# Four decoder layers in one kernel: weighing two head pairs at a time, a feed-forward in rounded halves, and a rotation that reads PSUM first

## Chip, cores and metric

One core of a Trainium2 chip runs the whole program in one launch. Its engines are TensorE (PE; its weight loads are shown as PEld), VectorE (DVE), ScalarE (ACT), GpSimd (POOL) and SyncE (SP, which here issues nearly all DMAs). Each works through its own list of instructions in order and waits on semaphores. The metric is the device time in microseconds.

## What is computed

Four cross-attention layers, one after the other, on x (16 samples of 100 rows of 256) against one context (16 samples of 361 rows of 256), all in fp32:

```python
x = L0(x, ctx)   # LayerNorm of x and ctx, 16 heads of 16, residual; then a feed-forward
x = L1(x, ctx)   # RMS norm of x, 16 heads of 64, residual
x = L2(x, ctx, mask)   # rotary keys and queries, mask, 16 heads of 64, residual, LayerNorm
x = L3(x, ctx)   # LayerNorm of x and ctx, 16 heads of 16, residual

# the feed-forward at the end of L0
y = layer_norm(x, ln2_g, ln2_b)
y = gelu(y @ w1 + b1)          # 256 -> 1024
x = x + (y @ w2 + b2)          # 1024 -> 256

# the rotation in L2, applied to keys and queries
x1, x2 = x[..., 0::2], x[..., 1::2]
r1, r2 = x1 * cos - x2 * sin, x2 * cos + x1 * sin
```

## The kernel before

The program has four parts in a row: `narrow_layer("L0")`, `feed_forward()`, `wide_layers()` for L1 and L2, `narrow_layer("L3")`. Between parts all engines meet.

**Products of halves.** A product of fp32 numbers is made of rounded halves in most places: an operand's high half is its value rounded to fp32r (ACT writes it), the low half is the rest (DVE subtracts), and PE sums high·high, high·low and low·high with moving operands in fp32r. Transposes, weighing and output projections take fp32 operands as they are; the trace shows each fp32 product as two records.

**Narrow part.** A slot (s, q) handles four heads of sample s: `turn(g-1, 0)`, `scores`, the jobs of list `a_`, `turn(g-1, 1)`, the jobs of `b_`. `jobs_at(s, q)` says which jobs: K, Q, V projections of the next samples, P (weighing), N, M, O (the way to the output). All jobs write into two banks PJ in turn, so job n waits until job n-2 has been read (`taken`). M is read by ACT (`L_OT<-PJ`), O by DVE (`X<-PJ,X`). On ACT a slot's order is: unload, two exponentials, `a_`, two exponentials, `b_`. On DVE: two maxima, the N job, unload, everything else.

**Feed-forward.** Groups of 4 samples (400 columns). PE makes the hidden layer from halves of W1 (line 972, 8 tiles of 128 rows, 6 products each), ACT applies gelu, PE makes the output with 100 rows of one sample as the stationary side and W2 in fp32 as the moving side (line 981, 8 products of 256 columns for each sample), ACT copies it, DVE adds it and the bias to X. A hardware loop runs over the groups; all of a group's hidden tiles come ahead of its output.

**Wide part.** 32 samples in a row (16 of L1, then 16 of L2) by 8 slots (s, p), a slot being two heads of 64. On PE a slot is: `scores(s, p)`, the jobs of `after_scores` (K of the next sample), `turn(g-1)` (transposes of the exponentials), `after_turn`, `weigh(g-2)`, `after_weigh`. Jobs share three banks. Q jobs exist in odd samples alone (two samples at a time), so samples come in pairs, an even one and an odd one. `scores` works on 64 rows, `weigh` on 64 columns of the array at a time. `weigh` of p = 0 and 4 must wait until `scale` (DVE, `wide_OT<-PS,wide_OT`, in slots 2 and 6) has read the bank PO. V is kept once, so V jobs wait for the weighings that read it.

In L2 each K and Q is rotated: ACT copies it out of PSUM (`wide_T`), DVE swaps neighbouring rows (`stream_shuffle`, into `wide_SH`), POOL makes two products (`wide_AC`, `wide_SH`), DVE adds them one slot later (`join`), ACT rounds the sum (`wide_KH`, `wide_QH`), DVE makes the low half (`wide_KL`, `wide_QL`). At p = 0 of each sample POOL also makes the tables of the next one (`tables`: mask times cos and sin). The raw context C has two slots, so SP loads two samples ahead.

## Time and profile before

| | |
|---|---|
| median of 3 runs | 2268.0 us (2266.34 to 2273.81) |
| the profiled run, its own time | 2268.11 us |
| its span in the profile | 2266.2 us, mean granted clock 0.963 |
| PE / PEld busy | 2062.2 us (91%) / 1678.8 us (74%) |
| DVE / ACT / POOL busy | 1425.7 us (63%) / 1263.5 us (56%) / 581.4 us (26%) |
| start of the parts, us | L0 0, feed-forward 370, wide 481, L3 1926 |

The span runs from the first to the last instruction of the profile. Busy PE time is not PE at its peak, since matmuls overlap: their pace is read from the distance of their starts. POOL's spans are rough. What stands in brackets or after "|" behind a row, with "<-", is the idle time of the engine ahead of it and who ended it.

### The profile page before, as it was taken

What the parts mean: (1) busy time and instruction counts of PE and PEld (TensorE: products, weight loads), DVE (VectorE), ACT (ScalarE), POOL (GpSimd) and SP (SyncE); (2) the same over time, 40 slices, a digit from 0 to 9 for tenths busy, and PEclk for the clock granted to TensorE, in tenths of its full rate; (3) what the DMA queues carried; (4) which work ended last, traced back from release to release, by engine and by line L of the source; (5) the groups of instructions that cost most, each with busy time, mean ns of one, the idle gap of its engine ahead of it and who ended that gap; (6) DMA issues with size and microseconds to landing.
All of it is one profiled execution on the core that took longest, in us unless ns stands there. A gap on an engine that the chain in (4) does not pass through costs nothing. (4 is left out here: it accounts for less than half of the span.)

```text
span 2266.2 us, 50658 instructions
## 1 busy us (share of the span) xinstructions
PE 2062.2 (91%) x18696; PEld 1678.8 (74%) x18696; DVE 1425.7 (63%) x2880; ACT 1263.5 (56%) x3225; POOL 581.4 (26%) x676
## 2 busy tenths in 40 slices
PE   6888986979999999999989999899999998889897
PEld 5777775867787787787767777777777776777776
DVE  5777774335445455454587777777777775577775
ACT  3677774335555555555555555555555554577775
POOL 3232320000000000000055655655556551000000
PEclk8999997989999999999999999999999999799999
DMA  6444332011000000000001000000000000344432
GB/s 170 135 136 139 117 122 82 0 52 58 14 8 8 14 8 15 8 8 14 9 15 35 15 9 9 9 9 15 9 9 10 1 1 1 115 121 121 121 122 71
DMA packets 72965, 109.69 MB, mean 48 GB/s; under 512 B 7062, under 2 KB 62618, under 8 KB 72730
## 3 DMA queue, kind: packets, MB, share of 16 engines
q1 hardware_dynamic: 72442, 105.98, 15.4%
q8 instruction: 155, 2.54, 0.5%
q14 instruction: 80, 0.66, 0.1%
q10 hardware_dynamic: 288, 0.51, 0.1%
HBM read 69.28 MB, written 37.19 MB: 47 GB/s over the span
## 5 line engine op out<-in xcount | busy, mean ns | idle before, releaser
L1444 ACT ACTIVATE wide_P<-PS,MX 100x361 f32<-100x361 f32 x512 | 288.9, 564 | 415.3 <-DVE MX L1562 411.4
L1562 DVE TENSOR_REDUCE MX<-PS 100x2 f32<-100x722 f32 x256 | 231.5, 904 | 181.4 <-PE PS L1312 181.3
L626 ACT ACTIVATE L_P<-PS,MX 100x361 f32<-100x361 f32 x512 | 253.5, 567 | 132.2 <-DVE MX L752 132.2
L752 DVE TENSOR_REDUCE MX<-PS 100x2 f32<-100x722 f32 x256 | 219.9, 900 | 48.3 <-PE PS L512 47.7
L1738 POOL TENSOR_TENSOR wide_AC<-wide_T,wide_COSM 128x362 f32<-128x362 f32 x128 | 118.0, 922 | 409.4 <-DVE wide_SH L1520 408.1
L1335 PE MATMUL PS<-wide_PT,wide_V 128*64 128x100 f32 (+1 forms) x3072 | 189.1, 257 | 29.6 <-issue 29.6
L524 PE MATMUL PP<-CON,L_P 100*128 100x100 f32 x1536 | 183.9, 257 | 26.6 <-DVE L_PT L759 20.7
L1335 PEld LDWEIGHTS PS<-wide_PT,wide_V 128*64 128x64 f32 (+1 forms) x3072 | 139.4, 136 | 84.4 <-issue 68.2
L524 PEld LDWEIGHTS PP<-CON,L_P 100*128 100x128 f32 x1536 | 151.5, 144 | 47.8 <-ACT L_P L626 34.3
L1321 PE MATMUL PP<-CON,wide_P 100*128 100x100 f32 x1536 | 179.6, 254 | 0.8 <-ACT wide_PT L1451 0.5
L1321 PEld LDWEIGHTS PP<-CON,wide_P 100*128 100x128 f32 x1536 | 164.6, 144 | 10.4 <-issue 2.0
L1418 ACT ACTIVATE wide_V<-PJ 128x512 f32<-128x512 f32 (+1 forms) x127 | 76.4, 601 | 153.7 <-PE PJ L1234 152.8
L1699 POOL TENSOR_TENSOR VE<-MV 128x2 f32<-128x2 f32 x8 | 2.5, 306 | 577.2 <-DVE MV L1615 577.2
L1234 PE MATMUL PJ<-wide_CTH,wide_WH 128*128 128x362 f32 x342 | 134.8, 394 | 2.9 <-DVE wide_KL L1515 1.6
L1739 POOL TENSOR_TENSOR wide_SH<-wide_SH,wide_SINM 128x362 f32<-128x362 f32 x128 | 133.8, 1045 | 0.0
L1568 DVE COPY wide_PT<-PP 128x300 f32<-128x300 f32 x256 | 116.6, 456 | 0.0
L1234 PE MATMUL PJ<-wide_WH,wide_CTH 128*128 128x512 f32 (+1 forms) x254 | 112.6, 443 | 4.2 <-ACT wide_T L1393 4.2
L1234 PE MATMUL PJ<-wide_CTH,wide_WL 128*128 128x362 f32 x342 | 116.0, 339 | 0.0
L1234 PE MATMUL PJ<-wide_CTL,wide_WH 128*128 128x362 f32 x342 | 115.9, 339 | 0.0
L759 DVE COPY L_PT<-PP 128x600 f32<-128x600 f32 x128 | 99.4, 777 | 18.6 <-PE PP L524 14.4
L1451 ACT ACTIVATE wide_PT<-PP 128x300 f32<-128x300 f32 x256 | 108.9, 425 | 0.6 <-PE PP L1321 0.6
L1532 DVE TENSOR_TENSOR wide_KL<-wide_AC,wide_KH 128x362 fp32r<-128x362 f32 x128 | 106.2, 830 | 0.9 <-ACT wide_KH L1401 0.3
(255 smaller groups left out, 5434.4 us busy)
## 6 DMA issues: line engine op xcount, KB each, us to landing
strips<-L_KS SPq DMA_DIRECT2D x256, 90.5 KB
L_KA<-strips SPq DMA_DIRECT2D x64, 362.0 KB, 3.1
C<-ctx_t SPq DMA_DIRECT2D x32, 361.0 KB, 3.1
kept<-L_CTH SPq DMA_DIRECT2D x16, 361.0 KB, 4.9
kept<-L_CTL SPq DMA_DIRECT2D x16, 361.0 KB, 5.5
L_CTH<-kept SPq DMA_DIRECT2D x16, 361.0 KB, 4.3
L_CTL<-kept SPq DMA_DIRECT2D x16, 361.0 KB, 5.1
C<-in_ctx SPq DMA_DIRECT2D x16, 256.0 KB, 3.4
```

Of the source, the lines that this page charges most:

```text
L524: last = nc.tensor.transpose(PPB[:, n, SQ * t:SQ * t + SQ], P[:, (4 * g + 2 * i + n) % 8, 128 * t:128 * t + 128], ident[0:SQ, 0:SQ])
L626: nc.scalar.activation(P[:, (4 * g + j) % 8, 0:SK], PSB[0:SQ, j, 0:SK], ACT.Exp, bias=MX[:, s % 2, 4 * q + j:4 * q + j + 1], scale=1.0).th ...
L752: nc.vector.tensor_reduce(MX[:, s % 2, 4 * q + 2 * i:4 * q + 2 * i + 2], PSB[0:SQ, 2 * i:2 * i + 2, 0:SK], AX.X, ALU.max, negate=True).the ...
L1234: last = nc.tensor.matmul(dst, l, r, start=n == 0, stop=n == len(todo) - 1)
L1321: last = nc.tensor.transpose(PP[i][:, SQ * t:SQ * t + SQ], P[:, (2 * g + i) % 4, 128 * t:128 * t + 128], ident[0:SQ, 0:SQ])
L1335: last = nc.tensor.matmul(PO[64 * i:64 * i + 64, SQ * at:SQ * at + SQ], V[0:r, 1024 * c + 64 * h:1024 * c + 64 * h + 64], PT[0:r, (2 * g + ...
L1444: nc.scalar.activation(P[:, (2 * g + i) % 4, 0:SK], PS_[i][0:SQ, 0:SK], ACT.Exp, bias=MX[:, s % 2, h:h + 1], scale=1.0, accum_out=DEN[:, s ...
L1451: nc.scalar.activation(PT[:, (2 * g + 1) % 4, :], PP[1][:, 0:KV_TILES * SQ], ACT.Copy).then_inc(Z["unloaded_odd"], 1)
L1562: nc.vector.tensor_reduce(MX[:, s % 2, 2 * p:2 * p + 2], PSB[0:SQ, 0:2, 0:SK], AX.X, ALU.max, negate=True).then_inc(Z["maxed"], 1)
L1568: nc.vector.tensor_copy(PT[:, (2 * g) % 4, :], PP[0][:, 0:KV_TILES * SQ]).then_inc(Z["unloaded_even"], 1)
L1738: nc.gpsimd.tensor_tensor(ac, src, c, ALU.mult)
L1739: nc.gpsimd.tensor_tensor(sh, sh, t, ALU.mult).then_inc(Z["rotated"], 1)
```

## The change

- **Narrow parts.** On ACT the M job is put ahead of a slot's exponentials. On DVE the O job is put ahead of the unload.
- **Feed-forward.** Unrolled; hidden tiles and output run as one stream, tile u of the hidden layer ahead of the output product of tile u-2. W2 and the gelu's result are split into halves too, the output is made transposed (256 rows of 400 columns, 6 products of 400 columns for each tile), gets its bias on ACT (`b2` is now a column vector), is transposed back (`back`) and added by DVE out of PSUM. W1's split is done in two halves.
- **Wide parts.** `weigh` runs in odd slots for two slots at once (g-3 and g-2), PT has 6 buffers in place of 4, `after_weigh` is gone and its V jobs are in other slots, O moves from p = 3 to 5. The wait for Wo moves from the start of the part to the first projection. C has one slot: SP loads context(s+1) once sample s has been split, so context(1) comes behind the load of L2's weights.
- **Rotation.** DVE swaps rows straight from PSUM, then ACT copies, then POOL makes both products and their sum. `post_stats` and `post` move from p = 4, 6 to 6, 7.

```diff
--- before.py
+++ after.py
+                        for key in a_:
+                            if key[0] == "M":
+                                job(key)
...
-                            job(key)
+                            if key[0] != "M":
+                                job(key)
...
                         for key in a_:
-                            if key[0] == "N":
+                            if key[0] in "NO":
                                 job(key)
                         if turns:
                             unload(g - 1)
                         for key in a_ + b_:
-                            if key[0] != "N":
+                            if key[0] not in "NO":
                                 job(key)
...
+                    def hidden(u):
+                        i, t = divmod(u, nf)
+                        pe.wait_ge(Z["w1_low"], 1 + 2 * t // nf)
+                        pe.wait_ge(Z["y_low"], KE * (i + 1))
+                        if u >= 2:
+                            pe.wait_ge(Z["hid_taken"], u - 1)
+                        c = slice(128 * t, 128 * t + 128)
+                        todo = [x for k in range(KE) for x in ((W1H[:, k, c], YH[:, i % 2, k, :]), (W1H[:, k, c], YL[:, i % 2, k, :]),
+                                                               (W1L[:, k, c], YH[:, i % 2, k, :]))]
+                        for m, (x, y) in enumerate(todo):
+                            last = nc.tensor.matmul(hid[u % 2][:, 0:GS], x, y, start=m == 0, stop=m == len(todo) - 1)
+                        last.then_inc(Z["hid_made"], 1)
+
+                    def output(u):
+                        i, t = divmod(u, nf)
+                        pe.wait_ge(Z["w2_low"], 1)
+                        pe.wait_ge(Z["hid_low"], u + 1)
+                        if t == 0 and i >= 2:
+                            pe.wait_ge(Z["out_taken"], KE * (i - 1))
                         for k in range(KE):
-                            bank = begin(i, n0 + k)
-                            for g in range(G):
-                                last = nc.tensor.transpose(bank[:, SQ * g:SQ * g + SQ], YN[:, g, 128 * k:128 * k + 128], ident[0:SQ, 0:SQ])
-                            last.then_inc(S["product"], 1)
-
-                    turn(0, 0, 0)
-                    pe.wait_ge(S["low_w"], 1)
-
-                    def body(i, last_group):
-                        pe.wait_ge(S["split"], i * KE + KE)
-                        for t in range(nf):
-                            bank = begin(i, HID + t)
-                            todo = [x for k in range(KE) for lh, ll in [[W[:, FF * k + 128 * t:FF * k + 128 * t + 128] for W in (WH, WL)]]
-                                    for x in ((lh, YH[:, k, :]), (lh, YL[:, k, :]), (ll, YH[:, k, :]))]
-                            for m, (x, y) in enumerate(todo):
-                                last = nc.tensor.matmul(bank[:, 0:G * SQ], x, y, start=m == 0, stop=m == len(todo) - 1)
-                            last.then_inc(S["product"], 1)
-                        if not last_group:
-                            turn(i, TURN, i + 1)
-                        pe.wait_ge(wo_in["ffn"], 16)
-                        pe.wait_ge(S["taken"], i * per + (HID + nf + nb))
+                            c = slice(128 * k, 128 * k + 128)
+                            for m, (x, y) in enumerate(((W2H, HH), (W2H, HL), (W2L, HH))):
+                                last = nc.tensor.matmul(outs[i % 2][k][:, 0:GS], x[:, t, c], y[:, u % 4, :], start=t == 0 and m == 0,
+                                                        stop=t == nf - 1 and m == 2)
+                        last.then_inc(Z["out_made"], 1)
...
+                    def back(i, half):
+                        pe.wait_ge(Z["out_taken"], KE * (i + 1))
+                        if i + 2 < groups:
+                            pe.wait_ge(Z["gained"], KE * (i + 2) + half + 1)
+                        else:
+                            pe.wait_ge(Z["added"], G * (i - 1) + 2 * half + 2)
+                        for v in range(2):
+                            g = 2 * half + v
+                            for k in range(KE):
+                                last = nc.tensor.transpose(turns[half][0:SQ, E * v + 128 * k:E * v + 128 * k + 128],
+                                                           OT[:, k, SQ * g:SQ * g + SQ], ident)
+                        last.then_inc(Z["back_made"], 1)
...
+                    for u, i, t in stream():
+                        if u < U:
+                            hidden(u)
+                        if u >= 2:
+                            output(u - 2)
+                        if i + 1 < groups and t in (3, 4):
+                            turn(i + 1, t - 3)
+                        if 0 < i < groups and t in (5, 6):
+                            back(i - 1, t - 5)
+                    for half in range(2):
+                        back(groups - 1, half)
...
+                    def hidden(u):
+                        act.wait_ge(Z["hid_made"], u + 1)
+                        if u >= 3:
+                            act.wait_ge(Z["hid_low"], u - 2)
+                        nc.scalar.activation(H32[:, u % 3, :], hid[u % 2][:, 0:GS], ACT.Gelu, bias=col("b1", u % nf)).then_inc(Z["hid_taken"], 1)
+                        act.wait_ge(Z["hid_taken"], u + 1)
+                        if u >= 4:
+                            act.wait_ge(Z["out_made"], u - 3)
+                        nc.scalar.activation(HH[:, u % 4, :], H32[:, u % 3, :], ACT.Copy).then_inc(Z["hid_high"], 1)
...
+                    stats(0)
+                    moments(0)
+                    split_w1(0)
                     normalise(0)
-                    split(0, 0, 0)
...
+                    split_w1(1)
+                    for k in range(KE):
+                        split(0, k)
+                    dve.wait_ge(Z["w2_high"], 1)
+                    nc.vector.tensor_tensor(W2L[:, :, :], w2, W2H[:, :, :].bitcast(fp32), ALU.subtract).then_inc(Z["w2_low"], 1)
...
-                after_scores, after_turn, after_weigh = [], [], []
+                after_scores, after_turn = [], []
                 if s + 1 < NS:
                     after_scores.append(("K", s + 1, p))
                 if s % 2 and s + 1 < NS:
                     after_turn.append(("X", s + 2, 0))
                 if p == 1 and s > 0:
                     after_turn.append(("R", s - 1, 1))
-                if p == 3 and s > 0:
+                if p == 5 and s > 0:
                     after_turn.append(("O", s - 1, 0))
                 if p == 5 and s < NS:
                     after_turn.append(("R", s, 0))
-                if p in (3, 4, 5) and s < NS:
-                    after_turn.append(("V", s, 3 + p - 3))
-                if p in (5, 6, 7) and s + 1 < NS:
-                    after_weigh.append(("V", s + 1, p - 5))
-                return after_scores, after_turn, after_weigh
-
-            SLOTS = [(s, p) for s in range(NS) for p in range(HP)] + [(NS, p) for p in range(4)]
+                if p in (2, 3, 4) and s < NS:
+                    after_turn.append(("V", s, 3 + p - 2))
+                if p in (6, 7) and s + 1 < NS:
+                    after_turn.append(("V", s + 1, p - 6))
+                if p == 0 and 0 < s < NS:
+                    after_turn.append(("V", s, 2))
+                return after_scores, after_turn
+
+            SLOTS = [(s, p) for s in range(NS) for p in range(HP)] + [(NS, p) for p in range(6)]
...
                     context(0)
-                    context(1)
                     load_output_weights(sp, "L1")
                     sp.wait_ge(Z["padded"], 1)
                     mask(B)
                     sp.wait_ge(Z["w_low"], 5)
                     load_weights(sp, "L2")
                     for s in range(NS):
-                        if s + 2 < NS:
+                        if s + 1 < NS:
                             sp.wait_ge(Z["c_low"], KE * (s + 1))
-                            context(s + 2)
+                            context(s + 1)
...
+                        if s == 0:
+                            pe.wait_ge(wo_in["L1"], 16)
...
-                        if 2 <= g <= HP * NS + 1:
+                        if g % 2 and 3 <= g <= HP * NS + 1:
+                            weigh(g - 3)
                             weigh(g - 2)
-                        for key in after_weigh:
-                            job(key)
 
...
-                        act.wait_ge(Z["made"], job_no[key] + 1)
+                        act.wait_ge(Z["shuffled"], r + 1)
                         if r >= NT:
                             act.wait_ge(Z["rotated"], r - NT + 1)
                         nc.scalar.activation(T32[:, r % NT, 0:n], bank(key)[:, 0:n], ACT.Copy).then_inc(Z["copied"], 1)
...
-                        dve.wait_ge(Z["copied"], r + 1)
-                        nc.vector.stream_shuffle(SH[:, r % NB, 0:n], T32[:, r % NT, 0:n], [q ^ 1 for q in range(32)]).then_inc(Z["shuffled"], 1)
-
-                    def join(key):
-                        n, r = (SKE if key[0] == "K" else 2 * SQ), turn_no[key]
-                        dve.wait_ge(Z["rotated"], r + 1)
-                        nc.vector.tensor_tensor(AC[:, r % NB, 0:n], AC[:, r % NB, 0:n], SH[:, r % NB, 0:n], ALU.add).then_inc(Z["joined"], 1)
+                        dve.wait_ge(Z["made"], job_no[key] + 1)
+                        nc.vector.stream_shuffle(SH[:, r % NB, 0:n], bank(key)[:, 0:n], [q ^ 1 for q in range(32)]).then_inc(Z["shuffled"], 1)
...
+                        shuffles_first = s + 1 < NS and rope(s + 1)
+                        if shuffles_first:
+                            for key in after_scores:
+                                job(key)
                         if p == 2 and s:
                             scale(s - 1, 1)
                         if p == 6 and s < NS:
                             scale(s, 0)
-                        for key in turns_of(g - 1):
-                            join(key)
...
-                        pool.wait_ge(Z["shuffled"], r + 1)
+                        pool.wait_ge(Z["copied"], r + 1)
...
                         nc.gpsimd.tensor_tensor(sh, sh, t, ALU.mult).then_inc(Z["rotated"], 1)
+                        pool.wait_ge(Z["rotated"], r + 1)
+                        nc.gpsimd.tensor_tensor(ac, ac, sh, ALU.add).then_inc(Z["joined"], 1)
```

ACT in a narrow part, the slot q = 3 of a sample in L3 (L_PT: unload, L_P: exponentials, L_OT: the M job). Before:

```order
2170 L633 ACTIVATE L_PT<-PP 128x600
2171 L626 ACTIVATE L_P<-PS,MX 100x361 x2
2172 L575 ACTIVATE L_OT<-PJ 128x200
2173 L575 ACTIVATE L_V<-PJ 105x16x16
2174 L626 ACTIVATE L_P<-PS,MX 100x361 x2
```

Now:

```order
2204 L622 ACTIVATE L_PT<-PP 128x600
2205 L564 ACTIVATE L_OT<-PJ 128x200
2206 L615 ACTIVATE L_P<-PS,MX 100x361 x2
2207 L564 ACTIVATE L_V<-PJ 105x16x16
2208 L615 ACTIVATE L_P<-PS,MX 100x361 x2
```

The eviction of M stands one place earlier, ahead of the first two exponentials.

PE in L2, slot p = 2 of an even sample, from the transposes to the next scores (wide_MNEG). Before:

```order
4415 L1321 MATMUL PP<-CON,wide_P 128x100 x6
4416 L1335 MATMUL PS<-wide_PT,wide_V 64x100 x6
4417 L1309 MATMUL PS<-wide_MNEG,wide_FILL 100x362 x2
4418 L1312 MATMUL PS<-wide_KH,wide_QH 100x362 x2
4419 L1312 MATMUL PS<-wide_KL,wide_QH 100x362 x2
```

Now:

```order
4607 L1395 MATMUL PP<-CON,wide_P 128x100 x6
4608 L1306 MATMUL PS<-wide_WH,wide_CTH 128x512
4609 L1306 MATMUL PS<-wide_WL,wide_CTH 128x512
4610 L1306 MATMUL PS<-wide_WH,wide_CTL 128x512
4611 L1306 MATMUL PS<-wide_WH,wide_CTH 128x512
4612 L1306 MATMUL PS<-wide_WL,wide_CTH 128x512
4613 L1306 MATMUL PS<-wide_WH,wide_CTL 128x512
4614 L1383 MATMUL PS<-wide_MNEG,wide_FILL 100x362 x2
```

The weighing that stood in slot 2 is gone to slot 3, and a V job stands in its place.

DVE in L2, slot p = 2 of an odd sample (wide_OT: scale; wide_AC: join). Before:

```order
1189 L1562 TENSOR_REDUCE MX<-PS 100x2
1190 L1584 TENSOR_TENSOR wide_OT<-PS,wide_OT 128x400
1191 L1525 TENSOR_TENSOR wide_AC<-wide_AC,wide_SH 128x362
1192 L1525 TENSOR_TENSOR wide_AC<-wide_AC,wide_SH 128x200
1193 L1520 STREAM_SHUFFLE wide_SH<-wide_T 128x362
1194 L1568 COPY wide_PT<-PP 128x300
1195 L1520 STREAM_SHUFFLE wide_SH<-wide_T 128x200
1196 L1532 TENSOR_TENSOR wide_KL<-wide_AC,wide_KH 128x362
1197 L1535 TENSOR_TENSOR wide_QL<-wide_AC,wide_QH 128x200
```

Now:

```order
1164 L1629 TENSOR_REDUCE MX<-PS 100x2
1165 L1592 STREAM_SHUFFLE wide_SH<-PJ 128x362
1166 L1651 TENSOR_TENSOR wide_OT<-PS,wide_OT 128x400
1167 L1635 COPY wide_PT<-PP 128x300
1168 L1592 STREAM_SHUFFLE wide_SH<-PS 128x200
1169 L1599 TENSOR_TENSOR wide_KL<-wide_AC,wide_KH 128x362
1170 L1602 TENSOR_TENSOR wide_QL<-wide_AC,wide_QH 128x200
```

Both joins are gone from DVE (POOL has them now), and the shuffle of K reads the PSUM bank and stands ahead of scale.

## Rows read from the trace of the kernel before

**Rows 1.** busy time by stretch: length, PE PEld DVE ACT POOL busy, clock, DMA.
```profile
516.00:1125.00 609.00, 601.53 (x4814) 480.01 (x4812) 304.67 (x600) 320.57 (x936) 12.65 (x32) 1.00 0.04 11
1175.00:1885.00 710.00, 654.74 (x5105) 527.85 (x5104) 529.35 (x1148) 380.07 (x1113) 415.17 (x443) 0.95 0.04 11
1362.81:1407.75 44.94, 40.99 (x321) 32.52 (x321) 33.52 (x67) 23.85 (x68) 24.35 (x25) 0.96 0.05 10
1407.75:1458.42 50.67, 47.47 (x366) 38.88 (x365) 37.77 (x91) 27.03 (x81) 31.62 (x37) 0.93 0.04 10
1377.28:1380.69 3.41, 3.41 (x17) 2.89 (x14) 3.41 (x4) 0.95 (x3) 1.80 (x2) 0.50 0.00 0
1408.00:1413.00 5.00, 5.00 (x49) 4.24 (x46) 4.52 (x12) 2.95 (x9) 4.86 (x5) 1.00 0.01 3
```

**Rows 2.** groups by line, narrow stages: what | busy, mean | idle before.
```profile
L372 PE MATMUL PJ<-L_CTH,L_WH 128*128 128x362 f32 x128 | 49.1, 384 | 24.9 <-ACT L_OT L575 23.7 <-DVE L_CTL L696 1.1
...
L372 PE MATMUL PJ<-L_XTH,L_WH 128*128 128x200 f32 x128 | 38.9, 304 | 23.1 <-DVE X L719 19.6 <-DVE L_XTL L696 2.4 <-DVE L_QB L700 0.8
```

**Rows 3.** timeline, last narrow stage: start, length, engine, what [idle before].
```profile
2062.91 1.02 ACT L626 ACTIVATE L_P<-PS,MX 100x361 f32<-100x361 f32 x2 [0.81 <-DVE MX L752]
2063.82 0.34 ACT L575 ACTIVATE L_OT<-PJ 128x200 f32<-128x200 f32 x1
...
2069.09 0.77 DVE L759 COPY L_PT<-PP 128x600 f32<-128x600 f32 x1
2069.78 0.41 DVE L719 TENSOR_TENSOR X<-PJ,X 100x256 f32<-100x256 f32 x1
```

**Rows 4.** timeline of PE in the feed-forward, first group of samples.
```profile
388.13 0.34 PE L972 MATMUL PP<-ffn_YH,ffn_WH 128*128 128x400 f32 x1
...
388.31 0.34 PE L972 MATMUL PP<-ffn_YL,ffn_WH 128*128 128x400 f32 x1
...
398.35 3.40 PEld L981 LDWEIGHTS PS<-WO,ffn_HT 128*100 128x100 f32 x16
```

**Rows 5.** timeline: first and last of the feed-forward block.
```profile
370.75 1.91 ACT L989 ACTIVATE ffn_WH<-W_RAW 128x2048 fp32r<-128x2048 f32 x1 [1.93 <-PEq L280]
...
383.55 0.69 PE L972 MATMUL PS<-ffn_YH,ffn_WH 128*128 128x400 f32 x1 [2.09 <-DVE ffn_YL L1038]
...
481.41 1.06 ACT L1372 ACTIVATE wide_WH<-W_RAW 128x1024 fp32r<-128x1024 f32 x1 [1.21 <-PEq L936]
```

**Rows 6.** timeline and DMA list: start of the wide stage.
```profile
485.95 0.61 DVE L1623 TENSOR_SCALAR wide_XN<-X,RS 100x256 f32<-100x256 f32 x2
...
489.89 0.93 PE L1264 MATMUL PJ<-CON,wide_XN 100*128 100x100 f32 x4 [10.12 <-DMA WO<-in_L_xattn_wo]
...
515.99 0.89 ACT L1380 ACTIVATE wide_CTH<-C 128x361 fp32r<-128x361 f32 x2
...
W_RAW<-in_L_xattn_Wq SPq DMA_DIRECT2D x1, 1024.0 KB, 10.3
```

**Rows 7.** timeline of PE, layer 1: one weighing, then scores.
```profile
801.01 0.74 PE L1335 MATMUL PS<-wide_PT,wide_V 128*64 128x100 f32 x12
801.68 0.41 PE L1312 MATMUL PS<-wide_KH,wide_QH 64*100 64x362 f32 x2
```

**Rows 8.** groups by line, 15 samples of layer 2: waits and rotation.
```profile
L1739 POOL TENSOR_TENSOR wide_SH<-wide_SH,wide_SINM 128x362 f32<-128x362 f32 x120 | 125.1, 1042 | 0.0
...
L1532 DVE TENSOR_TENSOR wide_KL<-wide_AC,wide_KH 128x362 fp32r<-128x362 f32 x121 | 100.9, 834 | 0.7
...
L1335 PE MATMUL PS<-wide_PT,wide_V 128*64 128x100 f32 x960 | 67.7, 261 | 24.5 <-issue 24.5
...
L1309 PE MATMUL PS<-wide_MNEG,wide_FILL 64*100 64x362 f32 x240 | 50.8, 415 | 24.9 <-ACT wide_P L1444 24.9
...
L1739 POOL TENSOR_TENSOR wide_SH<-wide_SH,CON 128x200 f32<-128x200 f32 x57 | 42.1, 739 | 0.0
```

**Rows 9.** groups by line, 15 samples of layer 1: the same subtraction without GpSimd.
```profile
L1515 DVE TENSOR_TENSOR wide_KL<-PJ,wide_KH 128x362 fp32r<-128x362 f32 x78 | 41.7, 535 | 65.1 <-ACT wide_KH L1385 65.1
```

294 lines of the change are left out of this document (159 added, 135 removed).

## The prediction

> **What bounds the kernel now.** I read the page's busy times first: PE is busy 91% of the span, DVE 63%, ACT 56%, POOL 26%. Then the windows by stage [rows 1]. In 15 samples of layer 1, PE works 601.5 of 609.0 us at full clock and POOL almost not at all: only shorter PE work helps there. In 15 samples of layer 2, 710.0 us go by for nearly the same products. The difference has three places: PE idles 24.5 us ahead of weighings and 24.9 us ahead of scores [rows 8], and the granted clock is 0.95; part of each sample is at 0.50, the 1.2 GHz level [rows 1]. A mean of 0.95 is a tenth of the time at half speed, which costs about 35 us. An even sample took 44.9, an odd one 50.7 us. For narrow stages and feed-forward I read groups by line and the timeline: which wait ends last ahead of PE.
>
> **Narrow stages.** PE's K and Q products idle behind two readers of their bank, 23.7 us behind ACT's copy of M and 19.6 behind DVE's add of O [rows 2]: 43.3 us in 32 samples, 1.35 each. The timeline shows why [rows 3]. ACT waited 0.81 us for the maximum, ran two exponentials, and only then copied M. The copy (0.34 us) can now start when that wait began, at 2062.91 - 0.81 = 2062.10, 1.7 us earlier, and costs the exponentials nothing as long as M is made before the maximum. On DVE O's add (0.41 us) stood behind an unload of 0.77; it will end about 0.7 us earlier, and the unload and the turn that waits for it 0.4 later, a turn that comes later in PE's list. All 43.3 would be the upper end. Next late are exponentials and maxima, which these swaps don't make faster, so I take three quarters: **-32**; range -20 (only M's wait, less a little) to -43.
>
> **Feed-forward.** The block takes 481.41 - 370.75 = 110.7 us [rows 5]. Its hidden products start 0.18 us apart; the output of one sample takes 3.40 us [rows 4], so 13.6 per group of four, and nothing overlaps it. Now each tile has 6 hidden and 6 output products of 400 columns: a group is 8 x 12 x 0.18 = 17.3 us, and about 2.0 for 16 transposes there and back (four took 0.93 [rows 6], less in a row). Four groups make 77.2. ACT has two passes for each tile and DVE one, each of 400 columns; one tile lasts 2.18 us on PE, so both are hidden, by the lead of two tiles. If one tile's ACT work were over 2.18 us, 32 times the excess would show. The start: the first product came 12.8 us in [rows 5], behind a whole split of W1 (1.91 us on ACT, as much on DVE) ahead of the statistics. Half a split and statistics first give back about 4: 8.6. The end gets longer by the way back (copy, transposes, add): about 4.0 in all. W2's split stands on ACT and DVE before the first output, two tiles behind. 8.6 + 77.2 + 4.0 = 89.8: **-21** (-17 to -23).
>
> **Start of the wide stage.** PE waits 10.12 us for Wo and goes at 489.89, while x was normalised at 485.95 + 0.61 = 486.56 [rows 6]; 3.3 us can go. But context(1) now stands in SP's queue behind 3 MB of weights, each of which took 10.3 us to land [rows 6]. They are issued near 502.5; I put the landing at 513 to 514.5, and ACT would want it at 515.99 - 3.3 = 512.7. Up to 1.8 us comes back: **-1.5** (-3.3 to +2).
>
> **Layer 1.** A weighing takes 801.68 - 801.01 = 0.67 us with entry and exit of its column mode [rows 7]; two take 1.34. Entry and exit are now paid once for two weighings, and products change to them once instead of twice. What that is worth no row shows by itself; it lies between 0 and 0.67 us a pair, and I estimate 0.24, a third of one weighing, since most of the 0.67 must be its 12 records: 0.24 x 4 a sample, 15 us a layer. The V product no longer follows a weighing, and V jobs fill slots in which PE waited for the softmax: I take 0.6 us a sample, another 9. **-24** (-15, if only the pairing counts at my price, to -26). In this layer DVE and ACT have half their time free (304.7 and 320.6 of 609 us [rows 1]).
>
> **Layer 2.** (a) Pairing as in layer 1: -24. (b) In slot 2 the weighing waited for `scale`; 24.5 us in 15 samples [rows 8], 26 in 16. It now comes a slot later, with a V job between: -26. (c) The joins. DVE loses them, which it needn't (529 of 710 us busy). POOL gets a third pass. Its price isn't in the trace: the nearest row is the second product, 1.04 us for K and 0.74 for Q [rows 8], same sizes and operands, and I take these. Below it the subtraction of the same size on an engine with free ports, 0.53 [rows 9]; above it, 2.0 if an add of two late operands waits for DVE each time. POOL's work goes from 24.4 to 24.4 + 8 x 1.04 = 32.7 us in an even sample and from 31.6 to 31.6 + 8 x 1.78 = 45.9 in an odd one. PE's floor (length less clock loss, less 3.3 of waits, less 1.6 by (a)) is about 38 even and 42 odd. So POOL is the bound of odd samples, by some 4 us, and not of even ones. Inside a sample the queue is uneven: at p = 0 the tables take 4.86 of 5 us [rows 1], and K and Q of p = 0 to 2 stand behind them. What waits is ACT's rounding, and ACT is in order: its next exponentials stand behind it, and PE's scores behind these. Placing the passes one after another by these durations, I get a stall of 2.3 to 2.9 us near p = 3 in each sample, where PE idles 24.9 / 15 = 1.7 us now [rows 8]: with odd samples' excess +15. (d) The shuffle out of PSUM takes a copy out of the chain, which shortens it, and frees the bank later, which three banks cover: 0. (e) The clock: what stands before each half-clock stretch is idle PE. One idle place of the two goes, one stays, so I leave the dips: 0, with up to -35 if they vanish. Sum **-35**; range +20 (joins at 1.5 and 1.1: odd samples near 52) to -75.
>
> In trace rows the same subtraction into KL takes 834 ns beside a busy POOL [rows 8] and 535 without [rows 9]. The Trainium skill has a rule that speaks against the joins: "Perfetto Trace Analysis", section "Optimizing Scalar/DVE Operations", says that GpSimd and DVE share a read port of SBUF, so that work moved between them might not help; "SBUF — State Buffer", section "Who interferes with whom", says that a DVE instruction with two SBUF inputs contends with a GpSimd one that reads SBUF. The rows agree with it.
>
> **The last samples** of the wide stage lose two weighings' entries: -1. **Sum**: -32 - 21 - 1.5 - 24 - 35 - 1 = -114.5. The profiled run's span is 2266.2 us with 1.9 outside it; its 2268.11 is the median 2268.0. 2266.2 - 114.5 + 1.9 = 2153.6: **2154 us**.
>
> **Rivals.** *B: POOL's queue takes layer 2's gain.* With POOL busy 39 of 47 us a sample instead of 28, each subtraction with two SBUF operands meets it more often: the 0.30 us between 834 and 535 [rows 8, 9] came at a share of 415 / 710 = 0.58, and 0.83 would make it 0.43; POOL's passes grow alike, to about 1.3 and 0.95, and odd samples stay near 50. Layer 2 gains nothing: 2154 + 35 = **2189**. For it: POOL is the bound of odd samples even at my price. Against: DVE reads memory less often itself (no joins, shuffles from PSUM). This is what the Trainium skill's rule on the shared port would give. *C: both stalls and the dips go.* If POOL's queue is drained before anyone waits, layer 2 runs at layer 1's pace and clock, -95 instead of -35: about **2095**. For it: one idle place of two goes for certain. Against: the tables at p = 0. *E: the swaps in the narrow stages only move the wait* to the scores: -10 there, about **2176**. For it: exponentials and maxima hold PE elsewhere already. *D: slower.* The one mechanism is the price of the joins. Everything outside layer 2 gives -79.5, so layer 2 must lose that much, 10.6 us a pair of samples. With even samples at 43, an odd one must reach 63, which is 31.6 + 8 x 3.9: the joins of K and Q must cost 3.9 us together, where the rows give 1.78. At 2.5 and 1.8 us the odd sample is 66.0, the pair 109 against 95.6, 7.5 pairs lose 100: **2289**. Only a pass twice as dear as its neighbour does it.
>
> **Chances.** A (the forecast) 0.50, B 0.20, C 0.17, E 0.08, D 0.05. The forecast's own terms spread over 2130 to 2175. The range 2100 to 2210 takes in B and E with their spread and half of C; left out are half of C, the far end of B and D, under 2 in 10. Faster by over 0.3% (about what a measurement of this kernel can tell from no change): A, C, E and all of B but 0.02, so 0.93; within 0.3%: 0.02 of B, 0.01 of D, so 0.03; slower: 0.04.
>
> **What the new profile would show.** Narrow: the idle time of K and Q products behind the copy of M and the add to X gone; if it names the exponentials instead, E. Feed-forward: output products 0.18 us apart, block near 90 us. Wide start: no wait for Wo, and ACT's first split of context(1) released by a DMA. Layer 1: 24 weigh records in about 1.1 us, two samples in 78.5 where 609 / 7.5 = 81.2 are now. Layer 2: the wait ahead of weighing gone; POOL's third pass near 1.04 and 0.74 us; ACT's rounding released by POOL, scores late near p = 3 once a sample; odd samples 45.6 to 48.3, even 42.9 to 44.4; dips at 0.50 still there. The forecast fails most easily on the join's price and on the clock.

## The result and the profile after

| | before | changed |
|---|---|---|
| median | 2270.7 us (4 runs) | 2143.1 us (4 runs, 2141.1 to 2145.4) |
| span of the profiled run, mean clock | 2266.2 us, 0.963 | 2139.7 us, 0.975 |

The ratio is 0.944, with a 95% interval of 0.9417 to 0.9462. The forecast was 2154 us. The parts, each from one profiled execution of either kernel; a sample begins with its first scores product, and sample 15 is the last of layer 1:

| part | forecast, us | measured, us |
|---|---|---|
| first narrow stage | -16 | 370.75 to 353.75: -17.0 |
| feed-forward | -21 | 110.7 to 90.9: -19.7 |
| start of the wide stage, to sample 0 | -1.5 | 33.97 to 32.28: -1.7 |
| layer 1, samples 0 to 14 | -24 (16 samples) | 609.7 to 589.2: -20.5 |
| samples 15 to 30 | -35 (layer 2, 16 samples) | 760.2 to 700.7: -59.5 |
| the rest with the last narrow stage | -17 (-16 and -1) | 381.0 to 372.8: -8.2 |

The windows of the changed kernel are first layer 1, then layer 2, then an even and an odd sample of layer 2 (length, then PE, PEld, DVE, ACT, POOL busy, clock, DMA). They answer to [rows 1].

```profile
477.00:1066.00 589.00, 582.57 (x4813) 474.68 (x4812) 305.51 (x600) 321.31 (x937) 12.59 (x32) 0.99 0.04 11
1114.00:1767.00 653.00, 610.64 (x5106) 499.52 (x5106) 456.26 (x966) 376.60 (x1111) 538.29 (x620) 1.00 0.05 13
1375.49:1417.24 41.75, 38.46 (x322) 31.02 (x321) 27.84 (x55) 23.17 (x68) 30.43 (x34) 1.00 0.06 12
1417.24:1463.08 45.84, 43.35 (x368) 35.96 (x366) 33.74 (x77) 27.27 (x84) 42.29 (x52) 1.00 0.04 10
```

Two samples of layer 2 take 87.6 us where 95.6 were, and the clock there is 1.00 where it was 0.95. POOL is busy 42.3 us of an odd sample.

Groups of PE, both narrow stages together, beside [rows 2]:

```profile
L361 PE MATMUL PJ<-L_CTH,L_WH 128*128 128x362 f32 x128 | 49.5, 387 | 4.9 <-DMA L_CTL<-kept 3.7 <-DVE L_CTL L689 1.1
...
L361 PE MATMUL PJ<-L_XTH,L_WH 128*128 128x200 f32 x128 | 39.1, 305 | 11.9 <-DVE X L712 6.7 <-DVE L_XTL L689 2.6 <-DVE L_QB L693 1.6
```

The wait behind ACT's copy of M is gone, that behind O's add is 6.7 instead of 19.6 us. 3.7 us behind a DMA (`L_CTL<-kept`) are new, all in the last stage. The exponentials are hardly named more than before: PE's transposes idle 6.9 us behind them where it was 4.2.

Feed-forward and the start of the wide stage, timeline, beside [rows 4 to 6]:

```profile
353.75 2.00 ACT L1016 ACTIVATE ffn_W1H<-W_RAW 128x1024 fp32r<-128x1024 f32 x2 [1.93 <-PEq L269]
...
363.09 0.67 PE L958 MATMUL PJ<-ffn_YH,ffn_W1H 128*128 128x400 f32 x1 [2.10 <-DVE ffn_YL L1089]
...
368.08 0.34 PE L970 MATMUL PS<-ffn_HH,ffn_W2H 128*128 128x400 f32 x1
...
368.26 0.34 PE L970 MATMUL PS<-ffn_HL,ffn_W2H 128*128 128x400 f32 x1
```

```profile
444.67 1.06 ACT L1444 ACTIVATE wide_WH<-W_RAW 128x1024 fp32r<-128x1024 f32 x1 [2.45 <-PEq L936]
...
450.20 0.90 PE L1336 MATMUL PJ<-CON,wide_XN 100*128 100x100 f32 x4 [6.85 <-DVE wide_XN L1690]
```

Output products are 0.18 us apart like the hidden ones; the first hidden product comes 9.34 us in (12.8 before; I had put 8.6), and the block ends at 444.67. In the wide stage PE no longer waits for Wo, but for x. ACT's split of context(1) starts at 477.55 with no idle time ahead of it, so the DMA wait that I had named as a sign isn't there.

A pair of weighings in layer 1, beside [rows 7], takes 1.19 us, where two single ones took 1.34:

```profile
794.55 1.26 PE L1409 MATMUL PS<-wide_PT,wide_V 128*64 128x100 f32 x24
795.74 0.41 PE L1386 MATMUL PS<-wide_KH,wide_QH 64*100 64x362 f32 x2
```

Layer 2, groups by form: GpSimd's third pass for K and Q, the subtraction, ACT's rounding, the mask product ahead of scores, beside [rows 8]:

```profile
L1811 POOL TENSOR_TENSOR wide_AC<-wide_AC,wide_SH 128x362 f32<-128x362 f32 x120 | 122.1, 1017 | 9.4
...
L1811 POOL TENSOR_TENSOR wide_AC<-wide_AC,wide_SH 128x200 f32<-128x200 f32 x57 | 37.3, 655 | 4.5
...
L1599 DVE TENSOR_TENSOR wide_KL<-wide_AC,wide_KH 128x362 fp32r<-128x362 f32 x121 | 93.4, 771 | 76.4 <-ACT wide_KH L1473 76.4
...
L1473 ACT ACTIVATE wide_KH<-wide_AC 128x362 fp32r<-128x362 f32 x120 | 61.1, 509 | 12.6 <-POOL wide_AC L1811 12.6
...
L1383 PE MATMUL PS<-wide_MNEG,wide_FILL 64*100 64x362 f32 x242 | 49.5, 398 | 41.7 <-ACT wide_P L1516 41.7
```

The third pass costs 1.02 and 0.66 us, where I had taken 1.04 and 0.74 from the second pass. An even sample takes 41.8 us (forecast: 42.9 to 44.4), an odd one 45.8 (45.6 to 48.3). The 24.5 us ahead of the weighing are gone, and the wait ahead of scores has grown from 24.9 to 41.7 us. One such wait, in slots 2 and 3 of an even sample:

```profile
1385.28 0.41 PE L1383 MATMUL PS<-wide_MNEG,wide_FILL 64*100 64x362 f32 x2 [0.58 <-ACT wide_P L1516]
...
1385.51 0.96 POOL L1811 TENSOR_TENSOR wide_AC<-wide_AC,wide_SH 128x362 f32<-128x362 f32 x1
...
1386.50 0.51 ACT L1473 ACTIVATE wide_KH<-wide_AC 128x362 fp32r<-128x362 f32 x1 [1.47 <-POOL wide_AC L1811]
...
1387.04 0.75 DVE L1599 TENSOR_TENSOR wide_KL<-wide_AC,wide_KH 128x362 fp32r<-128x362 f32 x1 [2.76 <-ACT wide_KH L1473]
...
1387.71 0.89 DVE L1629 TENSOR_REDUCE MX<-PS 100x2 f32<-100x722 f32 x1
...
1388.64 0.56 ACT L1516 ACTIVATE wide_P<-PS,MX 100x361 f32<-100x361 f32 x1 [0.93 <-DVE MX L1629]
...
1390.44 0.41 PE L1383 MATMUL PS<-wide_MNEG,wide_FILL 64*100 64x362 f32 x2 [1.11 <-ACT wide_P L1516]
```

GpSimd's sum ends at 1386.47. ACT has waited 1.47 us for it, rounds, and only then can DVE subtract, after 2.76 us of nothing. The next maximum stands behind that subtraction on DVE: its scores had begun at 1385.28 and the maximum comes at 1387.71. So the exponentials are late, and the next scores by 1.11 us.

### The profile page after: what moved, and what is told of

It is laid out like the page before. It is cut to its first block and busy times, and to the rows that moved or that the text cites. A ratio compares the mean times of both kernels' runs of the same rounds, so it can differ in the third digit from the quotient of the medians.

```text
span 2139.7 us, 50608 instructions
## 1 busy us (share of the span) xinstructions
PE 1984.0 (93%) x18664; PEld 1642.6 (77%) x18664; DVE 1358.2 (63%) x2706; ACT 1269.3 (59%) x3249; POOL 720.1 (34%) x868
## 3 DMA queue, kind: packets, MB, share of 16 engines
q8 instruction: 157, 2.57, 0.5%
## 5 line engine op out<-in xcount | busy, mean ns | idle before, releaser
L1811 POOL TENSOR_TENSOR wide_AC<-wide_AC,wide_SH 128x362 f32<-128x362 f32 x192 | 172.0, 896 | 15.1
L1395 PEld LDWEIGHTS PP<-CON,wide_P 100*128 100x128 f32 x1536 | 160.3, 141 | 10.2 <-issue 2.8
L1409 PE MATMUL PS<-wide_PT,wide_V 128*64 128x100 f32 (+1 forms) x3072 | 160.9, 253 | 0.0
L1599 DVE TENSOR_TENSOR wide_KL<-wide_AC,wide_KH 128x362 fp32r<-128x362 f32 x128 | 97.9, 765 | 79.8 <-ACT wide_KH L1473 79.8
L1809 POOL TENSOR_TENSOR wide_SH<-wide_SH,wide_SINM 128x362 f32<-128x362 f32 x128 | 140.4, 1097 | 0.0
L1306 PE MATMUL PJ<-wide_CTH,wide_WH 128*128 128x362 f32 x340 | 130.5, 384 | 0.8 <-DVE wide_KL L1587 0.7
L1306 PE MATMUL PJ<-wide_WH,wide_CTH 128*128 128x512 f32 (+1 forms) x258 | 108.2, 420 | 0.0
```

The source lines that it names most:

```text
L1306: last = nc.tensor.matmul(dst, l, r, start=n == 0, stop=n == len(todo) - 1)
L1395: last = nc.tensor.transpose(PP[i][:, SQ * t:SQ * t + SQ], P[:, (2 * g + i) % 4, 128 * t:128 * t + 128], ident[0:SQ, 0:SQ])
L1409: last = nc.tensor.matmul(PO[64 * i:64 * i + 64, SQ * at:SQ * at + SQ], V[0:r, 1024 * c + 64 * h:1024 * c + 64 * h + 64], PT[0:r, (2 * g + ...
L1809: nc.gpsimd.tensor_tensor(sh, sh, t, ALU.mult).then_inc(Z["rotated"], 1)
L1811: nc.gpsimd.tensor_tensor(ac, ac, sh, ALU.add).then_inc(Z["joined"], 1)
```

## The experiments

Where a table gives stretches, they are those of the parts above: samples 0 to 14, and 15 to 30.

Each ratio is to executions of the kernel before that were taken together with that kernel; their medians were 2267.5, 2273.3 and 2274.1 us, so medians of different rows are comparable to a few microseconds.

| kernel | median, us | ratio to before, 95% interval | 0 to 14 | 15 to 30 |
|---|---|---|---|---|
| before | 2270.7 | | 609.7 | 760.2 |
| changed | 2143.1 | 0.944 (0.9417 to 0.9462) | 589.2 | 700.7 |
| narrow swaps alone, on before | 2246.7 | 0.9881 (0.9838 to 0.9924) | 609.0 | 765.3 |
| M alone, on before | 2258.0 | 0.9965 (0.9933 to 0.9997) | 610.1 | 762.6 |
| swap from PSUM alone, on before | 2220.8 | 0.9773 (0.971 to 0.9835) | 609.1 | 708.0 |
| changed, weighings apart | 2173.4 | 0.9575 (0.9548 to 0.9602) | 609.5 | 707.3 |
| changed, one weighing a slot | 2146.5 | 0.9463 (0.9436 to 0.9489) | 600.7 | 695.2 |
| changed, sums on DVE | 2116.8 | 0.9313 (0.9298 to 0.9329) | 593.1 | 671.5 |
| changed, sum twice on GpSimd | 2238.1 | 0.9856 (0.9838 to 0.9875) | 592.0 | 792.0 |
| changed, swap out of the copy | 2187.7 | 0.9619 (0.9596 to 0.9641) | 589.2 | 738.5 |
| changed, Q's sum on DVE | 2141.0 | 0.9419 (0.9403 to 0.9435) | 590.6 | 695.2 |
| sums on DVE, weights in small pieces | 2110.2 | 0.9295 (0.9237 to 0.9353) | 586.9 | 670.6 |
| the same, tables early | 2103.4 | 0.9265 (0.9205 to 0.9325) | 585.9 | 666.3 |
| the same, single weighing in layer 2 | 2106.3 | 0.9285 (0.9226 to 0.9344) | 586.8 | 668.9 |

**The narrow swaps.** Kernel before, plus the hunks on ACT and DVE:

```diff
                         if turns:
                             unload(g - 1)
+                        for key in a_:
+                            if key[0] == "M":
+                                job(key)
...
-                            if key[0] == "N":
+                            if key[0] in "NO":
```

> The kernel before with the two swaps of the narrow stages alone. The prediction says -32 (about 2236 us). The changed kernel's trace already shows -17 in the first narrow stage and about -9 in the last one, where 3.7 us are waits for a DMA (L_CTL<-kept): by it -26, about 2242. The rival that the swaps only move the wait gives -10, about 2258.

> The kernel before with the M job ahead of the exponentials on ACT, and O left where it was. If the two waits add up, this takes away the 23.7 us behind L_OT and leaves the 19.6 behind X: about -15, 2254 us. If O's late add makes good for it (one wait in the place of the other), the idle time behind X grows to 30 or more and the time falls by under 6.

PE's groups of the first kernel:

```profile
L372 PE MATMUL PJ<-L_CTH,L_WH 128*128 128x362 f32 x128 | 49.6, 387 | 8.3 <-DMA L_CTL<-kept 7.0 <-DVE L_CTL L700 1.1
...
L372 PE MATMUL PJ<-L_XTH,L_WH 128*128 128x200 f32 x128 | 37.8, 295 | 11.6 <-DVE X L723 6.4 <-DVE L_XTL L700 2.6 <-DVE L_QB L704 1.6
```

and of the second:

```profile
L372 PE MATMUL PJ<-L_CTH,L_WH 128*128 128x362 f32 x128 | 49.1, 383 | 2.0 <-DVE L_CTL L700 1.1 <-DMA L_CTL<-kept 0.8
...
L372 PE MATMUL PJ<-L_XTH,L_WH 128*128 128x200 f32 x128 | 39.5, 308 | 26.1 <-DVE X L723 21.7 <-DVE L_XTL L700 2.5 <-DVE L_QB L704 0.8
```

Both swaps gave 1.2% of 2267, 27 us (17 to 37); in the trace 11 in the first stage and 13.3 from the last samples on. The changed kernel's trace had led me to expect 26. M alone gave 8 us (1 to 15) by the ratio, a third of the vanished 23.7 us of wait; in its one trace the two narrow parts are 14 us shorter. That lies between what I expected if the waits add up (15) and if one takes the other's place (under 6). O's wait stayed, at 21.7. So the waits don't replace each other, but only a part of each is gained. With both swaps the last stage waits 3.7 to 7.0 us for the DMA of the kept context. Lengths of the first stage differ between kernels with the same code there (353.75 in the changed kernel, 356.62 with the sums on DVE), so single microseconds of it are not to be read.

**Weighing.** In the changed kernel, apart:

```diff
                         for key in after_scores:
                             job(key)
+                        if g % 2 and 3 <= g <= HP * NS + 1:
+                            weigh(g - 3)
                         if 1 <= g <= HP * NS:
                             turn(g - 1)
...
-                            weigh(g - 3)
                             weigh(g - 2)
```

and one in each slot:

```diff
-                        if g % 2 and 3 <= g <= HP * NS + 1:
-                            weigh(g - 3)
+                        if 2 <= g <= HP * NS + 1:
                             weigh(g - 2)
```

> The changed kernel with the two weighings of an odd slot apart: the first one ahead of the transposes, the second one at the slot's end. Everything else stands where it stood. If sharing the entry and exit of the column mode is what pays, it costs 1.34 - 1.19 us for the weighing and about 0.15 for the transposes or V product beside it: 0.3 x 4 x 32 = 38 us where nothing hides it, and 25 to 38 with layer 2's waits: 2168 to 2181. If the other places of V, O and weighing are what pays, under +8: 2143 to 2151.

> The changed kernel with one weighing in every slot, two slots back, as before the change; the other jobs stay in their new places. This brings back single weighings (+25 to +38) and the wait for scale in slots 2 and 6 of layer 2 (+26). If that wait's idle time is what lowered the granted clock in the kernel before, the clock of layer 2 falls from 1.00 to about 0.95 again, for 30 us more: about 2235. If the joins on DVE had lowered it, the clock stays at 1.00: about 2205.

The first expectation was met in its number (2173.4 of 2168 to 2181), but the second run shows that its reason was wrong. One weighing a slot was to cost 60 us or more; it costs 3 us in all, inside the noise. In layer 1 two samples take 79.7 us (81.9 before, 78.5 changed): 1.24 us by pairing, 0.155 for each of 8 pairs, and 2.1 by what else the change does there, the new places of V and O above all. In layer 2 single weighing is 5.5 us faster, in one trace of each. The wait for `scale` doesn't come back: ahead of the weighings PE waits 2.5 us in 15 samples (24.5 before), with a V job now ahead of the weighing in slot 2. The clock stays at 1.00; that the sums on DVE had lowered it, as this branch of the expectation says, is not so either, since below it is 1.00 with the sums on DVE. Apart but in the same slot is 30 us worse, 2.5 in two samples of layer 1: the first weighing then stands ahead of the transposes. Both of these runs have single weighings, and they differ by 1.3 us in two samples of layer 1: the place of a weighing counts for about as much as sharing its entry and exit.

**The rotation.** Sums back on DVE:

```diff
...
                         if p == 6 and s < NS:
                             scale(s, 0)
+                        for key in turns_of(g - 1):
+                            join(key)
...
                         nc.gpsimd.tensor_tensor(sh, sh, t, ALU.mult).then_inc(Z["rotated"], 1)
-                        pool.wait_ge(Z["rotated"], r + 1)
-                        nc.gpsimd.tensor_tensor(ac, ac, sh, ALU.add).then_inc(Z["joined"], 1)
```

> The changed kernel with both sums of the rotation on DVE again, one slot later, behind scale; the rest of the change stays. If POOL's queue makes the 5.8 us that scores still wait in two samples of layer 2, they shrink and the time falls by 10 to 16: about 2130. If DVE's own order is worse (DVE stands in order behind POOL's products, and the unload of the weights stands behind it), the waits grow and the clock may fall with them: 2155 to 2180.

Groups of DVE, ACT and PE in layer 2:

```profile
L1604 DVE TENSOR_TENSOR wide_KL<-wide_AC,wide_KH 128x362 fp32r<-128x362 f32 x113 | 68.7, 608 | 14.4 <-ACT wide_KH L1473 11.6
...
L1597 DVE TENSOR_TENSOR wide_AC<-wide_AC,wide_SH 128x362 f32<-128x362 f32 x112 | 62.5, 558 | 2.3 <-POOL wide_SH L1816 2.3
...
L1473 ACT ACTIVATE wide_KH<-wide_AC 128x362 fp32r<-128x362 f32 x112 | 56.9, 508 | 0.0
...
L1383 PE MATMUL PS<-wide_MNEG,wide_FILL 64*100 64x362 f32 x226 | 46.2, 400 | 13.0 <-ACT wide_P L1516 11.6 <-issue 0.8
```

ACT's rounding of K waits for nothing now. DVE's subtraction waits 14.4 us in 14 samples, where it was 76.4 in 15. The wait ahead of scores is 13.0 us in place of 41.7, and the run is 26 us faster than the changed kernel, where I had expected 10 to 16. The sum costs DVE 0.56 us, where GpSimd needs 1.02. This confirms what the traces said of the chain, and gives the size: the sums on GpSimd cost layer 2 29.2 us. The same edit for Q alone:

```diff
+                        for key in turns_of(g - 1):
+                            if key[0] == "Q":
+                                join(key)
```

> The changed kernel with the sum of K on GpSimd and that of Q on DVE. GpSimd falls from 42.3 to about 37.5 us in an odd sample. If its load in odd samples bounds them, they fall by 1 to 2 us: 2127 to 2135. If the waits come from the queue's order behind the tables, or from DVE, nothing: 2140 to 2148.

GpSimd's busy time in an odd sample fell to 39.2 us, but the time by only 2 us (5.5 in the stretch): the odd sample grew to 46.5 us (from 45.8), the even one shrank to 40.5 (from 41.8). Less load on GpSimd didn't shorten odd samples, which speaks for the other reading: what counts is how long K's sum takes to reach DVE. The run doesn't part the two cleanly, since DVE now stood 17.4 us in 14 samples in front of Q's sum, waiting for GpSimd's product. The reverse, one more pass of the same size, ahead of the sum:

```diff
+                        nc.gpsimd.tensor_tensor(DUMMY[:, 0:n] if key[0] == "K" else DUMMY[:, 0:n].rearrange("p (v q) -> p v q", v=2), ac, sh, ALU.add)
                         nc.gpsimd.tensor_tensor(ac, ac, sh, ALU.add).then_inc(Z["joined"], 1)
```

> The changed kernel with a fourth pass on GpSimd: each sum is written once more, into a tile that nobody reads (extra work). With the sums at 0.9 (K) and 0.6 us (Q), GpSimd has 30.4 + 7.2 = 37.6 us in an even sample of 41.8 and 42.3 + 12 = 54.3 in an odd one of 45.9. If its queue bounds, an odd sample grows to about 54.5 and an even one little: +8 to +10 a pair, +65 to +80 in all, about 2215. If its queue isn't what bounds, under +20.

```profile
1416.95:1464.94 47.99, 42.03 (x320) 33.57 (x320) 27.52 (x55) 24.54 (x71) 42.23 (x49) 0.93 0.05 10
1464.94:1516.38 51.44, 44.51 (x366) 36.20 (x365) 32.87 (x76) 27.19 (x80) 50.18 (x61) 1.00 0.03 9
```

(Windows of an even and an odd sample.) It cost 95 us, more than expected, and the even sample grew as well, by 6.2 us, with GpSimd at 42.2 of 48.0 us and the clock at 0.93. The extra pass adds about 1.03 us to GpSimd's load and the same to the way of each K sum to ACT, so this run shows that the time is sensitive to GpSimd, but not by which of the two; in odd samples GpSimd is busy 50.2 of 51.4 us.

The swap out of the copy again:

```diff
-                        act.wait_ge(Z["shuffled"], r + 1)
+                        act.wait_ge(Z["made"], job_no[key] + 1)
...
-                        dve.wait_ge(Z["made"], job_no[key] + 1)
-                        nc.vector.stream_shuffle(SH[:, r % NB, 0:n], bank(key)[:, 0:n], [q ^ 1 for q in range(32)]).then_inc(Z["shuffled"], 1)
+                        dve.wait_ge(Z["copied"], r + 1)
+                        nc.vector.stream_shuffle(SH[:, r % NB, 0:n], T32[:, r % NT, 0:n], [q ^ 1 for q in range(32)]).then_inc(Z["shuffled"], 1)
```

> The changed kernel with the rows swapped out of ACT's copy again in place of out of PSUM; order and joins as changed. The prediction priced this part at 0: 2143 to 2148. The rival: DVE's shuffle now waits behind an exponential and the copy (about 1 us a slot), ahead of its unload, so that scores and transposes come later: +15 to +30, 2158 to 2173.

DVE's groups show the wait (the load of the mask stands right ahead of each swap), 157.4 us for 168 swaps, about 1 us each; PE's show it ahead of scores:

```profile
L1592 DVE LOAD_MASK_SELECT wide_SH<-wide_T x168 | 2.3, 14 | 157.4 <-ACT wide_T L1465 157.4
...
L1383 PE MATMUL PS<-wide_MNEG,wide_FILL 64*100 64x362 f32 x226 | 46.7, 403 | 58.4 <-ACT wide_P L1516 58.4
```

It cost 45 us by the medians and 38 in the stretch, more than the 15 to 30 expected. And alone, in the kernel before. The three waits are turned round as in the change, and the swaps are moved ahead of `scale` on DVE, so that source and order change together; the run above kept the order and changed the source alone:

> The kernel before with one part of the change alone: in layer 2 the rows are swapped straight from PSUM, ahead of scale, the sums and the unload on DVE, and ACT copies after that; the sums stay on DVE, weighing and V jobs stay where they were. If this part is what shortens the chain (38 us in the changed kernel), layer 2 loses 30 to 45 us and part of it is the granted clock, back near 1.00: 2225 to 2240. If the wait of the weighing for scale alone makes the idle stretches that the clock answers, the clock stays at 0.95 and the time falls by under 15: above 2253.

Windows of an even and an odd sample, columns as above:

```profile
1443.92:1486.32 42.40, 39.50 (x321) 31.28 (x320) 29.73 (x64) 24.38 (x68) 22.92 (x26) 1.00 0.05 11
1486.32:1531.72 45.40, 44.70 (x366) 36.41 (x365) 39.16 (x93) 27.76 (x81) 31.22 (x36) 1.00 0.04 11
```

This one edit took 52 us off layer 2 (37 to 66 us of the whole time by the ratio's interval) and brought its clock from 0.95 to 1.00, with weighing, V jobs and sums where they had been. The wait ahead of weighings fell with it, to 10.1 us in 14 samples.

**Faster than both.**

```diff
+                      (1, "Q", 0, 256), (1, "Q", 256, 512), (1, "Q", 512, 768), (1, "K", 0, 256), (1, "Q", 768, 1024), (1, "K", 256, 512),
...
+                    sp.wait_ge(Z["c_low"], KE)
+                    context(1)
                     sp.wait_ge(Z["w_low"], 5)
                     load_weights(sp, "L2")
```

> Sums on DVE (2117) and two more edits: layer 2's weights are split in 12 small pieces in place of 7, one a slot, and context(1) is loaded ahead of layer 2's weights. Sample 14 took 41.2 to 42.5 us where its like take 36.7, and sample 15 took 47.4 where its like take 41.8: 10 us by the split of large pieces. If those are stalls of DVE and ACT behind one large piece, half or more goes: 2107 to 2112. If it is the sum of the work, nothing: 2115 to 2119.

In the changed kernel sample 14 took 42.5 us, the even samples of layer 1 before it 36.7. The rows name the large piece of layer 2's weights: on DVE the next maximum stands behind 2.36 us of it, and PE's scores come 2.79 us late.

```profile
1036.15 1.91 ACT L1444 ACTIVATE wide_WH<-W_RAW 128x2048 fp32r<-128x2048 f32 x1
...
1038.09 2.36 DVE L1573 SCALAR_TENSOR_TENSOR wide_WL<-W_RAW,wide_WH 128x1024 fp32r<-128x1024 f32 x2 [1.27 <-ACT wide_WH L1444]
...
1040.36 0.90 DVE L1629 TENSOR_REDUCE MX<-PS 100x2 f32<-100x722 f32 x1
...
1043.00 0.62 PE L1386 MATMUL PS<-wide_KH,wide_QH 64*100 64x362 f32 x2 [2.79 <-DVE wide_KL L1587]
```

In small pieces samples 14 and 15 took 39.0 and 46.8 us (41.2 and 47.4 with the sums on DVE alone). That is 2.8 of the 7 us in the medians. This run has a second edit, the earlier load of context(1), and its trace is 5.9 us shorter from the start of the wide stage to the end of sample 0. But there the clock differs, 0.95 against 0.82 in sample 0, and the changed kernel, which loads late, took 33.7 us for that sample at 1.00. So the runs don't show a gain from the earlier load.

```diff
-                        if p == 0 and s + 1 < NS and rope(s + 1):
-                            tables(s + 1)
+                        if p in (4, 5, 7) and B <= s + 2 < NS:
+                            tables(s + 2, (4, 5, 7).index(p))
```

> As v1, and GpSimd makes the masked tables of a sample one sample earlier, in the slots 4, 5 and 7, into a second copy of the tables. If the tables at p = 0 make the 1.5 us of waits ahead of scores near p = 1 and 2 of an even sample, they go: 10 to 15 us less than v1, about 2097. If they come from elsewhere in the chain, the same as v1.

Samples 15 to 30 fell by 4.3 us (1.6 of it in sample 15), the median by 7, where 10 to 15 were expected: of the two waits near p = 1 and 2 one (0.8 us) stayed. In these two the intervals overlap; that both help is likely, not shown. The last edit weighs singly in layer 2, by the line of the table's one weighing a slot:

> As v2, with weighing in pairs in layer 1 and one by one, in every slot, in layer 2. With sums on GpSimd single weighing had given 5.5 us in layer 2 (695.2 against 700.7), since the waits there shrank. If that holds without those waits, 5 less than v2. If pairing is worth in layer 2 what it is in layer 1 once nothing waits (1.24 us a pair of samples), 10 more than v2.

Neither: the median is 3 us higher, but single times overlap (2104.1 to 2112.1 against 2100.0 to 2108.2). The traces have 2.6 us of it in samples 15 to 30, some 0.3 in each pair of samples. So pairing is worth little in layer 2 once little waits there, and the runs don't show that it is worth anything. 2103 us is 1.9% less than the changed kernel (0.9265 against 0.944).

## Why the prediction was right, and where it was not

**Direction, size and range** held: 2154 forecast, 2143 measured, of 2100 to 2210. But layer 2's terms were wrong, and their errors partly met. The stretches of samples 15 to 30 give them one after another: the swap from PSUM 760.2 to 708.0, -52 where 0 stood; weighings and V jobs in their new places 708.0 to 671.5, -36.5 where -50 stood; the sums to GpSimd 671.5 to 700.7, +29 where +15 stood. Two errors of 14 us took back half of one of 52, and the narrow stages another 8. (The terms were put for 16 samples; the stretches have 15 of layer 2.) That the total came within 11 us owes something to luck.

**Narrow stages.** The waits went as forecast; the value of three quarters was too high, -25 with the last samples of the wide stage in place of -33. In the last stage a DMA is late next, which no row of before named. Rival E had little of it: the wait behind exponentials grew by 2.7 us.

**Feed-forward** was read right: pitch, block of 90 us, start 9.3 us in.

**Wide start.** PE started 2.95 us earlier within the stage (5.53 us in instead of 8.48), of which 1.7 us were left at sample 0. It wasn't context(1)'s later load that took the rest back, as I had put it: ACT didn't wait for it. PE was busy 23.9 us instead of 21.8 for the same 118 records, at a mean clock of 0.77 against 0.87. So -1.5 was met by luck.

**Layer 1.** 78.5 us for two samples was forecast and measured, though from 81.9 us and not from the 81.2 that I had taken: 3.4 us less. The inside was wrong: I put 0.24 us on each shared entry, it is 0.155; the rest of the change, the jobs' places above all, gave the larger part. Sample 14 took 3.9 us more than before by the split of weights, which I hadn't costed. Sample 0 took 3.5 less, but at a clock of 1.00 against 0.95; with the sums on DVE, the same code there, it took 38.9 us at 0.82. So of the -20.5 a few microseconds are not the change's.

**Layer 2, (d), the failed step.** I priced the swap out of PSUM at 0, since it only shortened a chain. It is the largest single part of the change: 52 us alone, 38 if undone at the end. The error was to look at how many operations the chain has and not at who waits in it. DVE is in order; the swap waited for ACT's copy, which stood behind an exponential, which needs DVE's own maximum. Rows for it were there before the change: of 710 us DVE was busy 529, PE's scores waited for exponentials, 24.9 us [rows 8], and DVE stood 62.4 us in 15 samples in front of its swaps, 0.35 each, for ACT's copy:

```profile
L1520 DVE LOAD_MASK_SELECT wide_SH<-wide_T x177 | 2.3, 13 | 63.8 <-ACT wide_T L1393 62.4
```

**Layer 2, (e).** I left the clock dips where they were, since one idle place would stay. One stays, but its waits are shorter, at most 1.57 us in the steady samples of the changed kernel. In two samples of before, PE's idle time was 7.1 us and its busy time 88.5; with the swap alone 3.6 and 84.2. I put the 4.3 us of busy time down to the clock, for the same products, about 34 in all; the trace of before has two stretches at 0.50 in such a pair, 3.4 and 6.8 us long, the trace with the swap alone none. That is the 35 us that I gave to rival C. Its other half, waits that vanish, did not happen (41.7 us ahead of scores), so layer 2 lies between the forecast's -35 and C's -95, at -59.5.

**Layer 2, (a) and (b).** Pairing was to give 24 us as in layer 1; in layer 2 single weighing was 5.5 us faster, and 2.6 slower once the sums were on DVE. The wait for `scale` is gone, as forecast, but not by the pairing: one weighing a slot has 2.5 us of it, and the swap from PSUM alone had taken it from 24.5 to 10.1. That the V job in the slot does the rest is argued from the order, not tested by itself.

**Layer 2, (c).** The join's price was right for K (1.02 us, put at 1.04) and a little high for Q (0.66, put at 0.74), and there is a stall behind ACT's rounding; the sum, +15, was half of what it costs (29.2). I had reckoned with the queue's length after the tables and with POOL as the bound of odd samples, busy 45.9 us there; it was 42.3. By the rows above it is the latency of each K sum: DVE's next maximum stands behind a subtraction that needs it, in even samples also. That the sums on GpSimd cost 29 us is shown; that latency and not load makes all of it is read from the rows.

**Rival B** used the share of time in which GpSimd is busy to price the subtraction. That fell: with GpSimd busy 538 / 653 = 0.82 of layer 2 it took 771 ns, before, at 0.58, 834, and with the sums on DVE, at 374 / 585 = 0.64, 608. What meets what decides, not the share. The 535 ns of [rows 9] are not quite the same subtraction, as one of its inputs is a PSUM bank (`PJ`); but in layer 2, with both inputs in SBUF, it took as little as 516 ns too. The lines of all 128, before and after (least, median and most ns):

```profile
L1532 DVE TENSOR_TENSOR wide_KL<-wide_AC,wide_KH x128: 516/909/1180, 1135.1 to 1888.8; 128x362 fp32r<-128x362 f32 x128
...
L1599 DVE TENSOR_TENSOR wide_KL<-wide_AC,wide_KH x128: 524/577/1259, 1075.9 to 1771.0; 128x362 fp32r<-128x362 f32 x128
```

The Trainium skill, "Perfetto Trace Analysis", section "Optimizing Scalar/DVE Operations", warned that work moved between DVE and GpSimd might not help; this case agrees, 26 us to the worse, though what the rows show here is mostly order and latency, and not the port alone.

**Rival D** needed joins of 3.9 us together; they are 1.7.

## What to carry to other kernels

A step that waits on an in-order engine is priced by what stands behind it, not by its own length: a swap that waited 0.35 us for a copy (0.94 in the changed kernel with the swap out of the copy) held up unloads and maxima and, with them, the clock. Ahead of moving work from a half-busy engine to an idle but slower one, ask whether the result's consumer stands ahead of something on the critical path. When undoing single parts, undo each in turn: this change held one part worth -52 us and one that cost 29.
